# Moving the tail of a query-softmax layer, and keeping a turned context in DRAM between two cross attentions

## The reference, cut to what matters

```
x = x + L0_xattn(layernorm(x), ctx, ctx)     # 16 heads, first reader of ctx
x = x + L0_attn(layernorm(x))                # linear attention
x = x + L0_ffn(layernorm(x))                 # "query softmax", below
x = x + L1_xattn(layernorm(x), ctx, ctx)     # one head, second reader of ctx
x = x + L1_attn(layernorm(x))                # causal
x = x + L1_ffn(layernorm(x), ...)            # attention and 8 experts

L0_ffn:   scores = einsum('bqd,bkd->bkq', q, k) / sqrt(D); attn = softmax(scores, over q)
          z = l2n(heads @ Wo); z = l2n(z @ Wff); return gelu(z)
L1_xattn: q = x@Wq+bq; k = ctx@Wk+bk; v = ctx@Wv+bv; return softmax(q k^T) v
```

## Time and profile before

| what | value |
|---|---|
| median of 3 runs | 1531.38 us |
| the profiled execution's own time | 1534.49 us |
| its span | 1532.6 us |
| TensorE / VectorE / ScalarE / GpSimd busy | 1437.2 / 1093.7 / 927.5 / 284.3 us |
| first cross attention | to about 940 us |
| head pairs of the query softmax | 1005 to 1096 us |
| turn-over to the second cross attention | 1096 to 1133 us |
| second cross attention, both halves running | 1133 to 1285 us |

### The profile page before, as it was taken

One profiled execution on the slowest core, in us unless ns is written; L12 is line 12 of the kernel. 1 busy time (PEld: TensorE's weight loads), 2 busy tenths in 40 slices (PEclk: granted clock), 3 DMA queues, 4 the chain that ended last, 5 costly groups with the idle time before them and its releaser, 6 DMA issues.

```text
span 1532.6 us, 28387 instructions
## 1 busy us (share of the span) xinstructions
PE 1437.2 (94%) x11230; PEld 848.7 (55%) x11230; DVE 1093.7 (71%) x2254; ACT 927.5 (61%) x1899; POOL 284.3 (19%) x323
## 2 busy tenths in 40 slices
PE   7899999999999999999999997999789998888898
PEld 5355555555555455555455544655357778745565
DVE  4787777787777777777888844767767557757657
ACT  5367777777767677777777773257664442437621
POOL 3363222222212222222200003000110001220110
PEclk9899999999999999999999999999899999989999
DMA  6865553555545465554444205010001101166000
GB/s 179 174 141 111 107 99 75 104 115 106 99 90 102 85 120 99 106 92 84 98 90 77 49 1 184 18 38 1 21 1 56 56 1 39 46 122 128 2 1 28
DMA packets 90405, 120.56 MB, mean 79 GB/s; under 512 B 8288, under 2 KB 70368, under 8 KB 84320
## 3 DMA queue, kind: packets, MB, share of 16 engines
q1 hardware_dynamic: 90272, 118.74, 37.3%
HBM read 87.79 MB, written 30.93 MB: 77 GB/s over the span
## 4 chain that ended last, share of the span: by engine, by line
PE 73%; ACT 10%; DVE 10%; issue 4%; DMA 3%; POOL 1%; SPq 1%; DVEq 0%; ACTq 0%; POOLq 0%
PE psum L543 15%; PE psum L524 13%; PE psum L508 12%; ACT probs L763 4%; PE psum L571 3%; PE psum L1813 3%; PE psum L270 3%; PE psum L610 2%; PE psum L1795 2%; PE psum L2457 2%; DVE peaks L667 2%; PE psum L1409 2%; PE psum L279 1%; PE psum L2467 1%; PE psum L1802 1%
## 5 line engine op out<-in xcount | busy, mean ns | idle before, releaser
L667 DVE TENSOR_REDUCE peaks<-psum 128x1 f32<-128x512 f32 x1024 | 641.2, 683 | 193.2 <-PE psum L508 192.8
L763 ACT ACTIVATE probs<-psum 128x512 f32<-128x512 f32 x1024 | 525.6, 619 | 66.4 <-PE psum L524 62.6
L524 PE MATMUL psum<-queriesT,keysT 98*128 98x256 bf16 x2048 | 393.8, 274 | 7.9 <-ACT queriesT L824 3.1
L508 PE MATMUL psum<-keysT,queriesT 96*128 96x512 bf16 x1024 | 390.0, 384 | 8.1 <-DMA keysT<-key_parts 5.5
L524 PEld LDWEIGHTS psum<-queriesT,keysT 98*128 98x128 bf16 x2048 | 172.8, 99 | 202.7 <-ACT probs L763 83.1
L543 PE MATMUL psum<-probs,values 128*17 128x256 f32 x4096 | 245.9, 380 | 1.1 <-ACT probs L763 1.1
L543 PEld LDWEIGHTS psum<-probs,values 128*17 128x17 f32 x4096 | 107.2, 97 | 103.7 <-issue 26.8
L508 PEld LDWEIGHTS psum<-keysT,queriesT 96*128 96x128 bf16 x1024 | 98.6, 96 | 81.6 <-issue 50.9
L892 POOL CAST key_parts<-key_f 128x512 bf16<-128x512 f32 x57 | 34.7, 609 | 516.8 <-ACT key_f L794 509.9
L794 ACT ACTIVATE key_f<-psum,bk 128x512 f32<-128x512 f32 x59 | 40.5, 686 | 119.3 <-PE psum L571 119.2
L1843 DVE TENSOR_REDUCE peaks<-row_w 128x1 f32<-128x512 f32 x64 | 43.5, 682 | 53.9 <-ACT row_w L1901 53.9
(11 more groups left out here) (292 smaller groups left out, 1763.8 us busy)
## 6 DMA issues: line engine op xcount, KB each, us to landing
keysT<-key_parts SPq DMA_DIRECT2D x31, 768.0 KB, 7.7
key_parts<-key_parts SPq DMA_DIRECT2D x90, 256.0 KB
keysT<-key_parts SPq DMA_DIRECT2D x31, 512.0 KB, 10.0
ctx_nat<-in_ctx_dram SPq DMA_DIRECT2D x32, 256.0 KB, 3.1
keysT<-key_parts SPq DMA_DIRECT2D x31, 256.0 KB, 11.7
ctx_in<-in_ctx_dram SPq DMA_DIRECT2D x24, 256.0 KB, 6.0
qk_parts<-early_weights SPq DMA_DIRECT2D x24, 128.0 KB
q_parts<-q_parts SPq DMA_DIRECT2D x12, 128.0 KB
```

What stands on the lines that cost most here:

```text
L508: e.matmul(ps, self.queriesT[0:ROWS, u % 2, g * GH + j, t * P:(t + 1) * P], self.keysT[0:ROWS, i % RING, j, c * BANK:(c + 1) * BANK], star ...
L524: made = e.matmul(ps[:, j * S:(j + 1) * S], self.keysT[0:AUG, i % RING, j, kt * P:(kt + 1) * P], self.queriesT[0:AUG, u % 2, g * GH + j, : ...
L667: e.tensor_reduce(self.peaks[:, i % 2, pair, c:c + 1], k.ps(("max", n)), AX.X, ALU.max).then_inc(*self.peaked.up(n))
L763: e.activation(self.probs[:, t % RINGP, e2 * GH * S:(e2 + 1) * GH * S], k.ps(("scores", t, e2)), ACT.Exp).then_inc(*self.exped.up((t, e2)))
```

## The change

Two things.

1. The first cross attention writes each turned chunk of batches 1 to 3 to DRAM (`save ctx`), six slots after it turned it; the second reads them (`fetch_turned`, 4 DMAs of 512 KB per batch) into `ctx_T`. The turning of batches 1 to 3 on TensorE and its copies go. ScalarE, before it overwrites `ctxT`, waits for the saves of the batch before.
2. The query softmax's jobs get other slots, 42 of them in its own loop and 20 inside the next stage. Batch 0's context is turned in slots 33 to 36, behind the pairs, and copied by VectorE and ScalarE in turn. Gelu of half 0 moves from slot 26 to 31, gelu of half 1 stays at 44 but that slot now lies before the exp of the first cross tile. All products are done before the first cross score. Tiles 4 to 7 of the products are evicted by ScalarE. The residual adds move to GpSimd. `turn x` is copied by two engines; the context queries are made per batch (256 columns) and not per half (512). `turn weights` moves from s = 20..22 to s = 1..3.

```diff
@@ ContextAttention0.plan
+                    at(slot + 6, "save ctx", b, c)
@@ ContextAttention0.scalar, "turn ctx"
                     w.wait_ge(self.ctx_made, (b, c))
+                    if b >= 2:
+                        w.wait_ge(self.ctx_saved, (b - 1, CH - 1))
@@ ContextAttention0.sync
+                elif job == "save ctx":
+                    w.wait_ge(self.ctx_kept, (b, c))
+                    e.dma_start(self.ctx_dram[b, :, own], self.ctxT[:, own]).then_inc(*self.ctx_saved.up((b, c)))
@@ Later
+    def fetch_turned(self, e, w, b, pair):
+        own = slice(2 * pair * BANK, (2 * pair + 2) * BANK)
+        w.wait_ge(self.first.ctx_saved, (B - 1, CH - 1))
+        e.dma_start(self.ctx_T[:, b % 2, own], self.first.ctx_dram[b, :, own]).then_inc(*self.turned_in[b % 2][pair].up(b))
...
-        if (b == 0 or c % 2) != engine:
+        if c % 2 != engine:
@@ QuerySoftmaxAttention
-    SLOTS3 = PAIRS3 + 2
-    LATE = PAIRS3 + 29
+    SLOTS3 = PAIRS3 + 10
+    LATE = PAIRS3 + 30
@@ schedule
-        for t, slot in enumerate((14, 16, 22, 23, 33, 33, 38, 39)):
+        for t, slot in enumerate((14, 16, 22, 23, 35, 35, 37, 37)):
             at(slot, "products", t)
-            at(slot + (t >= 4), "squares", t)
-        for c, slot in enumerate((15, 17, 18, 19, 20, 21, 24, 25)):
+            at((slot, 37, 40)[t // 2 - 1 if t >= 4 else 0], "squares", t)
+        for c, slot in enumerate((33, 33, 34, 34, 36, 36, 36, 36)):
             at(slot, "turn ctx", c)
         for half, (factor, gelu, add, scale, turn, queries, offset) in enumerate((
-                (26, 26, (28, 29), 31, 32, 33, 36), (43, 44, (46, 47), 50, 53, 56, 58))):
+                (26, 31, (37, 38), 38, 39, (40, 40), 45), (43, 44, (48, 49), 52, 54, (56, 57), 60))):
@@ vector_slot, "add"
-                    w.wait_ge(self.gelued, t)
-                    e.tensor_tensor(k.x[:, t, :], k.x[:, t, :], self.y[:, t, :], ALU.add).then_inc(*k.x_ready.up(("ffn0", t)))
-                    w.wait_ge(k.x_ready, ("ffn0", t))
+                    w.wait_ge(self.added, t)
                     self.norm.statistics(e, w, t)
@@ scalar_slot
+            if job == "squares" and a[0] >= 4:
+                e.activation(l.xn[:, t, :], ps[:, 0:D], ACT.Square, accum_out=l.norm3[:, 1, 0, i:i + 1])...
+                e.activation(self.y[:, t, :], ps[:, D:2 * D], ACT.Copy)...
+                w.wait_ge(self.squared, ("y", t))
+                e.activation(l.xn[:, t, :], ps[:, D:2 * D], ACT.Square, accum_out=l.norm3[:, 1, 0, 4 + i:5 + i])...
+            elif job == "turn x" and a[1]:
+                e.activation(l.xnT[:, kk, half * BANK:(half + 1) * BANK], k.ps(("x4", half, kk)), ACT.Copy)...
@@ norm_half (GpSimd), between the power and norm_inverse
+        for t in range(4 * half, 4 * half + 4):
+            w.wait_ge(self.gelued, t)
+            e.tensor_tensor(k.x[:, t, :], k.x[:, t, :], self.y[:, t, :], ALU.add).then_inc(*w.up(self.added, t))
@@ QuerySoftmaxAttention.sync, ahead of the 8 fetch_ctx of batch 1
+        for pair in range(CH // 2):
+            l.fetch_turned(e, w, 1, pair)
@@ ContextAttention1.parts
-            if 20 <= s < 23:
-                yield "turn weights", s - 20
+            if 1 <= s < 4:
+                yield "turn weights", s - 1
...
-                c = s - (QT * CH * (b - 1) + 1)
-                if 0 <= c < CH:
-                    yield "turn ctx", b, c
+                c = s - (QT * CH * (b - 1) - 17)
+                if b >= 2 and c % 2 and 0 <= c < CH:
+                    yield "fetch turned", b, c // 2
@@ ContextAttention1.gpsimd: norm_half(1) first, then the bias of all eight tiles
```

More of the change, by code:

```diff
@@ L1026, in __init__ @@
         self.nat_in = [[k.landed(f"nat{r}_{c}_in") for c in range(CH // 2)] for r in range(2)]
-        self.nat_used = k.sem("nat_used")
+        self.turned_in = [[s.again() for s in first.first_in.values()], [s.again() for s in first.ctx_here + first.rows_here]]
     def wait_first(self, w):
@@ L1351, in schedule @@
                 at(turn, "turn x", half, kk)
-            at(queries, "context queries", half)
+            for n in range(2):
+                at(queries[n], "context queries", 2 * half + n)
             at(offset, "offset", half)
@@ L1363, in kept, with turned @@
         return self.k.kept(name, n) if n < (1 if name == "v3" else 2) else (self.k.kept_dve, (name, n))
+    def turned(self, half, kk):
+        return (self.xT_act if kk else self.offset_made), ("xT", half, kk)
     def banks_of(self, q):
@@ L1481, in tensor_slot @@
                 t, = a
-                ps = bank(("products", t), (self.y_kept, t))
+                ps = bank(("products", t), (self.squared if t >= 4 else self.y_kept, t))
                 w.wait_ge(self.folded, ("fold", "out"))
@@ L1493, in tensor_slot @@
                 half, kk = a
-                ps = bank(("x4", half, kk), (self.offset_made, ("xT", half, kk)))
+                ps = bank(("x4", half, kk), self.turned(half, kk))
                 for i in range(4):
@@ L1606, in vector_slot @@
                     e.tensor_copy(l.folded[:, D + 1:2 * D + 2], ps[:, 0:D + 1]).then_inc(*self.folded.up(("fold", name)))
-            elif job == "products":
+            elif job == "products" and a[0] < 4:
                 t, = a
@@ L1631, in vector_slot @@
                 l.keep_ctx(e, w, 0, a[0], 1)
-            elif job == "turn x":
+            elif job == "turn x" and a[1] == 0:
                 half, kk = a
@@ L1637, in vector_slot @@
             elif job == "context queries":
[L1638 to L1641, removed]
+                b, = a
+                w.wait_ge(k.projected, ("qc", b))
+                e.tensor_scalar(l.qcT[:, b * S:(b + 1) * S], k.ps(("qc", b))[:, 0:S], l.folded[:, D:D + 1], None,
+                                ALU.add).then_inc(*self.offset_made.up(("qc", b)))
             elif job == "offset":
@@ L1917, in gpsimd @@
         w.wait_ge(l.w4_in, 0)
[L1918 to L1924, removed]
+        l.ffn0.norm_half(e, w, 1)
+        for t in range(NT):
+            w.wait_ge(k.normed, ("xattn1", t))
+            w.wait_last()
+            e.tensor_tensor(k.x[:, t, :], k.x[:, t, :], l.b4_v[:, :], ALU.add).then_inc(*w.up(k.x_biased, ("xattn1", t)))
         for half in range(2):
@@ L1937, in sync @@
                 w.wait_ge(self.weighed, (QT * (b - 1) - 1, c))
-                w.wait_ge(k.turned, ("nat", b - 2, c))
                 l.fetch_ctx(e, b, c)
+            elif job == "fetch turned":
+                b, pair = a
+                w.wait_ge(self.scored, (QT * (b - 1) - 1, 2 * pair + 1))
+                l.fetch_turned(e, w, b, pair)
     def wait_left(self, w):
```

47 lines of the change are left out of this document (31 added, 16 removed).

## The result

The changed kernel takes 1525.94 us (median of 6 runs, 1524.54 to 1528.83) beside 1534.27 for the kernel before in the same rounds (6 runs, 1531.19 to 1540.28): ratio 0.9941, 95% interval 0.9924 to 0.9959, or 8.3 us less, where 10.1 less was forecast. Its profiled execution took 1524.63 us with a span of 1522.8 (before: 1534.49 and 1532.6). I had predicted 1521.3 for the median and 1524.4 for the profiled execution.

What follows compares the result with a forecast made beforehand. TensorE was taken as the bound, alone from 1137 to 1284.5 us. Head pairs -10.6, behind them +11.0, context turnings -10.1, half 1 -0.9, offset +0.5, saves 0: together -10.1, median 1531.38 to 1521.3 us, range 1511 to 1529.

Steps and rivals of the forecast that it cites:

- Part 1: Second cross attention: turned context read, not made; 23 groups of transposes leave TensorE, 10.1 us less, floor 5, ceiling 12.
- the 0.9 of half 1: Eight transposes of half 1 already done before the first weighing, 0.9 us less.
- the stretch: Second cross attention from first weighing to value projection; forecast to fall from 151.4 us to about 141.
- Saves and reads: 24 saves and 12 reads in SP's queue: cost zero, bounds 0 and +3 for the saves.
- Part 2: Head pairs, slots 14 to 31: context turnings out 4.2 us, gelu of half 0 out 6.4, together -10.6.
- T0: End of head pair 31, forecast to move from 1095.9 to 1085.3 us.
- Part 3: Work between T0 and the first weighing grows by 11.0 us; first weighing at T0 + 48.2, bounds -7 and +7.
- rival B: Between pairs and first weighing: VectorE reaches the first exp some 8 us earlier than queued; 1513 us, chance 0.22.
- the 8 to 10 given as a sign: A TensorE gap of 8 to 10 us before the first turn of cross rows would show the forecast right.
- Rival C: Start of cross attention loses to clock (+4 us) and VectorE's order (offset, +2): 1525 to 1529 us, chance 0.16.
- A: The forecast itself: -10 us, own range 1517 to 1526, chance 0.52.
- Table loads: ScalarE's table loads fall from four to two at 1.28 us each, saving 2.6 us, inside Part 2 and Part 3.

Runs made afterwards that it cites:

- part 1 alone: Kernel before plus only the saves, reads and removed turnings of batches 1 to 3, old schedule kept: 1525.53 us, ratio 0.9943.
- the tail alone: Changed kernel without saves and reads, batches 1 to 3 turned on TensorE as before, new query-softmax slots kept: 1533.31 us, ratio 0.9995 to the kernel before.
- copying first: Changed kernel with VectorE's weight-row copy of chunk s ahead of the maximum of chunk s + 11 in each second cross attention slot: 1519.64 us, ratio 0.9895.
- holding the bank: Changed kernel with the bank that sums a tile's weighed rows handed out again one slot later: 1521.9 us, ratio 0.9916.

## Why the prediction was right, and where it was not

**Part 1, -10.1: right in kind, a part given back.** The work left TensorE as counted: 23 x 0.437 and the 0.9 of half 1 make 11.0, the rows give 11.8. "TensorE stays the bound and the 10.1 us is taken whole" is the step that failed. With part 1 alone the stretch fell by 7.6 us, half the way to the named floor of -5 ("the context-free slots meet VectorE's queue oftener"), and TensorE's waits grew by 1.8. With the whole change it fell by 6.7 where 10.5 was forecast, and the waits grew by 5.1; with the tail alone they grew by 2.0. Why the two together have more waits than the sum of both stays open.

I had compared averages over eight slots (VectorE 1.4, ScalarE 1.1, TensorE 2.19). The rows that I had read show that ScalarE's load is not even: 4 us of exp in a row, once per tile. That a slot shorter by 0.43 leaves less slack to ride over it is my reading of the timeline; what the experiments show is the next link: copying first took 5.0 us of waits away, holding the bank 4.4, so both were orders and not loads.

**Saves and reads, 0: right.** The last eviction of the first stage starts at 927.8 us (928.1 before), DMA share 0.53 after 0.51, and the saves alone gave 1.0007, though with that stage 1.6 us longer in their profile. None of TensorE's waits in the stretch is for a read of turned context.

**Part 2, -10.6: right, measured -11.3.** The last exp of pair 31 begins at 1084.09, so T0 is near 1084.6 where 1085.3 was forecast; the gelu alone is 5.7 to 6.6 by its own experiment (6.4), the turnings 2.8 to 4.8 by theirs (4.2; the last pair of the changed kernel came at 1084.1 in one profile and 1082.1 in the other).

**Part 3, +11.0: measured +9.3.** In us behind T0, forecast and measured: first score 18.0 and 17.3; TensorE out of scores 28.3 and 27.8; gelu of half 1 done 23.9 and 22.1; first exp 35.8 and 33.1; TensorE's gap ends 37.9 and 35.3; first weighing 48.2 and 46.4. Absolute 1131.05 instead of 1133.5. So the first exp came 2.7 us earlier behind T0 than I queued it, 1.8 of them already there at the gelu's end: the direction of rival B but not its 8. The gap before the first turning of cross rows was 7.5 us, just under the 8 to 10 given as a sign. The tail alone (0.9995) agrees with parts 2 and 3 nearly cancelling.

**The clock.** It fell to 0.77 in the mean of 1101.9 to 1131. Behind the gap the four transposes took 1.09 instead of 0.60, two scores 1.92 instead of 1.02, five transposes of half 1 1.33 where eight of the context took 1.09 at full clock, four more 0.78 for 0.60: about 2.2 us where the sum had 0.7. Rival C's mechanism was there, at a third of its price. Its second term, which the sum has at +0.5, is the wait of 1.5 us behind the offset of half 1. C's range holds the result, and so does the top of A's (1526, by 0.06 us); but what the stretch fell short by is mostly the waits behind the exps and the sum's bank, which are in no term of either.

**Table loads.** Between the last pair exp (ends 1084.67) and the gelu (1086.08) lie 1.41 us with the load of 1.28 in them, as before. The Trainium skill (ScalarE: Activation LUTs, What ACT_TABLE_LOAD costs) has about 2.66 us with a drain; no row here shows the drain, so the measurement stands.

**Sum by rows, profiled executions.** First weighing -2.0 (forecast +0.4), stretch -6.7 (forecast -10.5), behind the value projection -1.1 (forecast 0): -9.8 us. The forecast missed by 0.2 us in the profiled execution, and that is luck: +3.8 in the stretch stands against -2.4 and -1.1 on either side of it; in the medians it missed by 4.6, of which 2.9 is the level of the kernel before (1534.27 in the comparison, 1531.38 in the runs I started from). As a ratio I forecast 0.9934, inside the measured interval of 0.9924 to 0.9959.

## What to carry to other kernels

When work leaves the engine that is the bound, compare the others not only by their mean over a period but also at their worst burst in it: here six of seven waits for the copy stood behind 4 us of exp, once in eight slots, although every mean had slack. Then look at what stands ahead of the awaited instruction on the engine that is late. Turning two instructions round there and giving a bank back one slot later brought more together than the change itself (0.9943 to 0.9853, with part 1 alone). A schedule that clears one stage by moving its work behind it should be costed to the first instruction that needs both: here 11.3 us gained in the pairs were followed by 9.3 lost behind them.

## What the runs showed of the hardware that I had not expected

The clock can fall in a stretch whose longest gap is 1.63 us, and need not. Slices of 10 us inside the head pairs, 1064 to 1094, of the tail alone and then of the kernel that copies first:

```profile
1064.00:1074.00 10.00, 8.58 (x68) 3.95 (x60) 6.96 (x15) 9.41 (x41) 1.64 (x1) 1.00 0.01 3
1074.00:1084.00 10.00, 8.32 (x72) 4.70 (x76) 7.17 (x16) 8.29 (x35) 0.00 (x0) 0.60 0.00 0
1084.00:1094.00 10.00, 10.00 (x73) 5.26 (x66) 4.37 (x13) 8.24 (x28) 1.23 (x2) 0.55 0.26 80
```

```profile
1064.00:1074.00 10.00, 8.37 (x77) 4.92 (x76) 8.01 (x17) 9.41 (x41) 1.64 (x1) 0.93 0.01 3
1074.00:1084.00 10.00, 8.49 (x60) 3.87 (x56) 5.32 (x11) 7.84 (x34) 0.00 (x0) 0.50 0.01 2
1084.00:1094.00 10.00, 10.00 (x58) 5.03 (x56) 3.98 (x10) 6.04 (x17) 2.92 (x4) 0.71 0.25 79
```

The changed kernel, which has the same instructions up to there as the one that copies first, kept 1.00 in both of its profiles; one of them:

```profile
1064.00:1074.00 10.00, 8.37 (x79) 4.50 (x80) 7.85 (x18) 9.41 (x42) 1.64 (x1) 1.00 0.01 3
1074.00:1084.00 10.00, 7.96 (x89) 4.44 (x85) 8.20 (x17) 9.97 (x46) 0.00 (x0) 1.00 0.18 54
```

Each fall follows the one gap of 1.63 us there, in which TensorE waits for VectorE's copy. The changed kernel has the same gap; the score group behind it takes 1.86 us in it, and 2.79 in the kernel that copies first, where the clock is falling. The changed kernel, then the one that copies first:

```profile
1072.09 1.07 PE L1446 MATMUL psum<-weights,v_scaled 128*32 128x256 f32 x16 [1.63 <-DVE early_weights L1594]
1073.09 1.86 PE L1432 MATMUL psum<-qT,kT 32*128 32x256 f32 x16
```

```profile
1070.85 1.07 PE L1446 MATMUL psum<-weights,v_scaled 128*32 128x256 f32 x16 [1.63 <-DVE early_weights L1594]
1071.86 2.79 PE L1432 MATMUL psum<-qT,kT 32*128 32x256 f32 x16
```

With turnings and gelu both out of the pairs all seven profiles have this gap, and the clock fell behind it in two. With the gelu out and the turnings in, two profiles have no such gap, and the clock held in both. What decides between two executions with the same gap isn't shown.

Executions of one kernel differ, and the longer ones have the lower mean clock: with the tail alone, seven at a mean clock of 0.981 took 1531.0 to 1533.6 us, three at 0.972 to 0.973 took 1538.6 to 1542.2. With the bank held, 0.981 to 0.984 went with 1516.5 to 1519.6 and 0.974 to 0.977 with 1524.2 to 1526.1. The profiled execution of these two lies 5.8 us above and 5.4 below its median; here the median of four to twelve executions with its ratio carried the verdicts, and the profiles the places.
